# A two-recurrence pipeline on one core: state halves in 32-column matmuls, gate biases seeded by ScalarE, the shared expert dealt in half tiles

## What is computed

```python
h = tanh(h @ Wh + (x_t @ Wx + b))                # L0, simple recurrence, h0 = cond
x = x + hs
h_bar = (x_t @ Wx + b) + h @ Wh                  # L1, gated recurrence: i, f, o, g
next_c = f * prev_c + i * g
next_h = o * tanh(next_c)
x = x + hs
out = sum over experts of w_be * mask * (gelu(x @ ew1 + eb1) @ ew2 + eb2)   # L2: routed, top 2 of 4
shared = gelu(x @ sw1 + sb1) @ sw2 + sb2
x = x + out + shared
x = x + adapter(x)                               # L3: low-rank weights made from cond
```

## Time and profile before

| | |
|---|---|
| median of 3 runs | 1195.59 us (1194.09 to 1197.45) |
| profiled execution | 1194.56 us |
| its span, first to last instruction | 1192.80 us |
| mean granted TensorE clock | 0.966 |
| TensorE matmuls busy | 1144.3 us (96%), 24138 instructions |
| VectorE busy | 887.2 us (74%) |
| ScalarE busy | 515.4 us (43%) |
| GpSimd busy | 403.5 us (34%) |

### The profile page before, as it was taken

The page is one execution under the profiler, slowest core; times in us unless marked ns, Lnnn a source line. Parts: engine busy times, 40 slices in busy tenths (PEclk is TensorE's granted clock), DMA queues, the critical chain, the costliest instruction groups (busy, mean ns, idle before and its releaser), DMA issues.

```text
span 1192.8 us, 58924 instructions
## 1 busy us (share of the span) xinstructions
PE 1144.3 (96%) x24138; PEld 1033.3 (87%) x24138; DVE 887.2 (74%) x3368; ACT 515.4 (43%) x1896; POOL 403.5 (34%) x1368
## 2 busy tenths in 40 slices
PE   5999999999999999999999999789999999999898
PEld 4889889889889889999999998678888888888677
DVE  6577888887887887787787778786666666666697
ACT  3344444444454444443444343323333333333476
POOL 2654454454454454454454440181000000000021
PEclk9658999999999999999999999899999999999899
DMA  8211202202112111110000000000000000000022
GB/s 242 73 40 43 78 4 79 78 5 79 48 36 79 32 51 27 15 15 11 4 4 5 4 4 4 2 1 2 2 2 2 2 1 2 2 2 2 4 75 85
DMA packets 43282, 37.17 MB, mean 31 GB/s; under 512 B 23128, under 2 KB 38794, under 8 KB 43020
## 3 DMA queue, kind: packets, MB, share of 16 engines
q1 hardware_dynamic: 42412, 33.12, 9.2%
q10 hardware_dynamic: 608, 0.30, 0.1%
HBM read 28.42 MB, written 4.98 MB: 28 GB/s over the span
## 4 chain that ended last, share of the span: by engine, by line
PE 86%; DVE 8%; ACT 2%; issue 2%; POOL 1%; DMA 1%; SPq 0%; DVEq 0%; POOLq 0%
PE bank L1087 17%; PE bank L1088 17%; PE bank L1089 17%; PE bank L1182 16%; PE bank L1188 8%; PE bank L1156 4%; DVE seq L742 2%; PE bank L1162 2%; PE bank L1238 1%; ACT tc L529 1%; DVE LH L789 1%; PE bank L1453 1%; PE bank L1228 1%; PE bank L1425 1%; DMA WE<-in_L_cond_b 1%
## 5 line engine op out<-in xcount | busy, mean ns | idle before, releaser
L1182 PE MATMUL bank<-LH,seq 128*128 128x16 f16 x8192 | 282.0, 170 | 12.4 <-DVE LH L789 11.0
L1182 PEld LDWEIGHTS bank<-LH,seq 128*128 128x128 f16 x8192 | 250.7, 96 | 43.9 <-DVE LH L789 32.2
L1087 PE MATMUL bank<-GH,WE 128*128 128x256 f16 x768 | 209.7, 273 | 6.6 <-DVE GH L771 6.3
L534 ACT ACTIVATE gel<-bank,seq 128x256 f32<-128x256 f32 x256 | 121.5, 475 | 217.3 <-PE bank L1089 217.1
L1087 PE MATMUL bank<-XHL,WE 128*128 128x256 f16 x768 | 210.2, 274 | 3.4 <-DVE XHL L752 3.2
L769 DVE CAST GH<-gel 128x256 f16<-128x256 f32 x384 | 122.1, 318 | 120.1 <-ACT gel L534 111.9
L1088 PE MATMUL bank<-XHL,WE 128*128 128x256 f16 x768 | 210.2, 274 | 0.0
L1089 PE MATMUL bank<-XHL,WE 128*128 128x256 f16 x768 | 210.2, 274 | 0.0
L1088 PE MATMUL bank<-GH,WE 128*128 128x256 f16 x768 | 209.5, 273 | 0.0
L1089 PE MATMUL bank<-GH,WE 128*128 128x256 f16 x768 | 209.5, 273 | 0.0
L518 ACT ACTIVATE tfig<-bank 128x96 f32<-128x96 f32 x256 | 64.2, 251 | 285.9 <-PE bank L1188 285.9
(11 more groups left out here) (184 smaller groups left out, 2599.5 us busy)
## 6 DMA issues: line engine op xcount, KB each, us to landing
stage<-in_L_cond_ew SPq DMA_DIRECT2D x8, 1024.0 KB, 8.7
stage<-in_L_cond_W SPq DMA_DIRECT2D x8, 1024.0 KB, 6.1
XHL<-in_x SPq DMA_DIRECT2D x8, 512.0 KB, 9.1
out<-WE SPq DMA_DIRECT2D x16, 256.0 KB, 2.2
stage<-in_L_cond_sw SPq DMA_DIRECT2D x2, 1024.0 KB, 5.3
scratch<-rows SPq DMA_DIRECT2D x96, 8.0 KB, 2.3
stage<-in_L_cond_Wx SPq DMA_DIRECT2D x1, 1024.0 KB, 9.0
stage<-in_L_cond_Wh SPq DMA_DIRECT2D x1, 1024.0 KB, 11.1
```

Of the source, the lines that this page charges most:

```text
L534: nc.scalar.activation(gel[:, m % 2, :], banks[m % len(banks)][:, 0:256], ACT.Gelu_apprx_tanh, scale=scale, bias=bias).then_inc(s["a_g"], 1)
L1087: MM(out_, w(HI), x(HI), start=start, stop=False, skip_group_check=True)
L1182: MM(z, LW[:, h, 1, c, tile * P:(tile + 1) * P], LH[:, old, HI, c], start=False, stop=False, skip_group_check=True)
```

## The change

- `rnn_step` on TensorE: the four products high weights x high state and the four high weights x rest become four matmuls of 32 columns that read both state halves at once and write them side by side in RB (index `a`). The step has 8 matmuls instead of 12. RB now holds 8 steps, not 16, and VectorE adds the two halves (`rnn_sum`, into `rz`) before ScalarE's tanh, which reads `rz`.
- `rnn_x` runs twice per block, for 8 steps each, at the start of the simple recurrence's steps 0 and 8; the splits of its input (`split_x`) move to steps 9, 11, 13, 14 (10 to 13 in the head).
- The gate biases come in a small table `gate_bias` (eight transfers of 512 bytes, scaled once on GpSimd). ScalarE copies them into a FIG or O bank after its last reader (`seed`), and the input parts after the first two turns begin without the bias matmul.
- `cell` is gone; `fc` takes c2 of the step before, and c2 takes the half.
- ScalarE does the cell's tanh before the simple recurrence's tanh pair.
- The shared expert is dealt out in half tiles of three matmuls (`HALVES`), ahead of the input parts in TensorE's order; the second O tile set moves from step 0 to steps 3 and 5.

```diff
             def rnn_step(blk, r):
...
-                for m in range(C):
-                    for c in range(C):
-                        for h in (HI, LO):
-                            MM(z[:, m, r], RW[:, h, 1, c, m * P:(m + 1) * P], RH[:, old, HI, c],
-                               start=False, stop=False, skip_group_check=True)
+                if r % G == 0 and n > 0:
+                    rnn_x(blk, r // G)
+                if n > 0:
                     pe.wait_ge(s["a_rh"], n)
+                for m in range(C):
+                    for c in range(C):
+                        MM(z[:, 0, m, r % G], RW[:, LO, 1, c, m * P:(m + 1) * P], RH[:, old, HI, c],
+                           start=False, stop=False, skip_group_check=True)
...
-                        last = MM(z[:, m, r], RW[:, HI, 1, c, m * P:(m + 1) * P], RH[:, old, LO, c],
+                        last = MM(z[:, :, m, r % G], RW[:, HI, 1, c, m * P:(m + 1) * P], RH[:, old, :, c],
                                   start=False, stop=(c == C - 1), skip_group_check=True)
...
+            def rnn_sum(n):
+                pair = RB[:, :].rearrange("p (a m t b) -> p m t b a", a=2, m=C, t=G)[:, :, n % G]
+                dve.wait_ge(s["pe_r"], n + 1)
+                V.reduce_sum(rz[:], pair, AX_X).then_inc(s["v_rz"], 1)
...
-                V.tensor_tensor(c2[:], fc[:], ig[:], ALU.add).then_inc(s["v_c2"], 1)
-                dve.wait_ge(s["v_c2"], n + 1)
-                V.tensor_scalar(cell[:], c2[:], 0.5, None, ALU.mult)
+                V.scalar_tensor_tensor(c2[:], fc[:], 0.5, ig[:], ALU.mult, ALU.add).then_inc(s["v_c2"], 1)
+                if rnn:
+                    rnn_sum(n + U)
                 dve.wait_ge(s["a_tc"], n + 1)
...
+            def seeds(it, u, last):
+                if u % H == H - 1 and not (last and u >= U - 2 * H):
+                    seed(it * U + u + 1, FIG[u // H % 2], slice(0, 6), H, "a_fig_seed")
+                if u % G == G - 1 and not last:
+                    seed(it * U + u + 1, OB[u // G], slice(6, 8), G, "a_o_seed")
...
                     lstm_gates(it, u)
+                    lstm_cell(it, u)
                     if not last:
                         rnn_step(it + 1, u)
-                    lstm_cell(it, u)
+                    seeds(it, u, last)
...
-                    if xr and u in (4, 6, 8, 10):
+                    if xr and u in (9, 11, 13, 14):
...
+HALVES = [0, 3, 2, 2, 2, 2, 2, 3, 0, 3, 2, 3, 2, 3, 2, 1]
+O_STEPS = (3, 5)
```

More of the change, by code:

```diff
@@ L892, in block_steps @@
                 for u in range(U):
-                    lstm_step(it, u)
+                    lstm_step(it, u, not last)
                     if last and u in extras:
@@ L899, in block_steps @@
                                 split_x2(it - 1, k)
-                        for kind, m in FILL[u]:
-                            if kind == "h":
+                        for kind, m, halves in FILL[u]:
+                            if kind == "h" and C - 1 in halves:
                                 split_g(it * M + m, m)
@@ L1190, in lstm_step, with hidden, down_, shared_hidden @@
                     last.then_inc(s[done], 1)
-            def hidden(tile, w, x, bank_, free):
-                free()
-                for c in range(C):
+            def hidden(tile, w, x, bank_, free, halves=range(C)):
+                if 0 in halves:
+                    free()
+                for c in halves:
                     last = three(bank_[:, 0:256], lambda h: w(h, c), lambda h: x(h, c), c == 0, c == C - 1)
-                last.then_inc(s["pe_h"], 1)
-            def down_(tile, j, w, first, last_, ybank):
-                pe.wait_ge(s["v_gl"], tile + 1)
-                for c in range(C):
+                if C - 1 in halves:
+                    last.then_inc(s["pe_h"], 1)
+            def down_(tile, j, w, first, last_, ybank, halves=range(C)):
+                if 0 in halves:
+                    pe.wait_ge(s["v_gl"], tile + 1)
+                for c in halves:
                     last = three(ybank[:, c * 256:(c + 1) * 256], lambda h: w(h, c),
                                  lambda h: GH[:, j % 4, h], first and c == 0, last_)
-                last.then_inc(s["pe_d"], 1)
-            def shared_hidden(blk, m):
+                if C - 1 in halves:
+                    last.then_inc(s["pe_d"], 1)
+            def shared_hidden(blk, m, halves=range(C)):
                 tile = blk * M + (M + m)
@@ L1232, in low_rank, with lstm_x @@
                     last.then_inc(s["pe_w2"], 1)
[L1234 removed]
+            def lstm_x(bank_, i, tile, group, steps, fresh):
                 n = (steps.stop - steps.start) * B
                 z = bank_[:, i * n:(i + 1) * n]
[L1238 to L1239 removed]
+                if fresh:
+                    MM(z, bias_pad[:, tile * P:(tile + 1) * P], ones_pad[:, 0:n], start=(i == 0), stop=False,
+                       skip_group_check=True)
                 for c in range(C):
@@ L1316, in block_steps @@
                         logits()
+                    if not first:
+                        for kind, m, halves in FILL[u]:
+                            if kind == "h":
+                                shared_hidden(it - 1, m, halves)
+                            else:
+                                shared_down(it - 1, m, halves)
                     if u == 0:
```

146 lines of the change are left out of this document (82 added, 64 removed).

## The result

The changed kernel takes 1203.22 us, median of 9 runs (1198.61 to 1206.61). The kernel before, run beside it, takes 1195.38 us, median of 9 (1192.45 to 1199.84). The ratio is 1.0055 [1.0032, 1.0077]: slower by 0.3 to 0.8%. The forecast was 1201.6.

The account below looks back on a forecast made before the run. Two close limits bound a step: TensorE's stream (2.36 or 2.56 us) and the state-write loop (2.45). Terms 4.9 + 0 + 6.4 - 4.9 - 0.4 = +6.0 us on 1194.56 gave 1200.6, 1201.6 as median; range 1184 to 1216.

Parts of the forecast that it names:

- the head: First 16 steps of the simple recurrence: VectorE's sum and splits start the gated recurrence at 56.0 instead of 51.09, +4.9 us.
- the loop: State write through TensorE, gate tanh and VectorE to the next state write: no step can be shorter than 2.45 us.
- The stream: TensorE's matmuls: 2.5 us per block leave; 37 us over 15 blocks is the most that could come.
- the rival of doubled cost: TensorE: 32-column matmuls cost double, nothing is saved, 0.1 us more in nine steps, +14, 1215 us; chance 0.03.
- Light blocks: Blocks without weight preparation: steps sum to 42.2 us against 43.1; blocks 9 to 14 together -4.9 us.
- The delay of the state write behind the input matmuls: Steps 0 and 8: state write queued behind the sum, which waits for fourteen 128-column matmuls; 0.34 us in step 0.
- Heavy blocks: Blocks 1 to 8, with weight preparation: 46.4 us each against 45.6, +6.4 us over eight blocks.
- Step 14: Blocks 1 to 8: input difference queued behind VectorE's wait for ScalarE's rounding; 4.77 us against 2.45, +2.32.
- Step 15: Blocks 1 to 8: 2.29 us on VectorE and the addition behind it 0.75, so 3.05, +0.49.
- The clock rival: Blocks 1 to 8: TensorE's wait in step 14 lowers the clock, +2 us a block, +16 in all, 1218; chance 0.12.
- The lighter stream is what counts: Gelu and splits come early enough: 41.0 us without weight preparation, 44.5 in blocks 1 to 8, about 1180; chance 0.20.
- The sum doesn't fit: VectorE's sum of the two halves takes over 0.45 us, +0.1 a step, 1225 us or more; chance 0.05.

Follow-up runs that it names:

- e2: Changed kernel with ScalarE's seeds issued behind the gelu of their step: 1203.38 us, ratio 1.0068 to the kernel before.
- e3: Changed kernel with block 0 of the simple recurrence using 12 matmuls of 16 columns, read directly by ScalarE without VectorE's sum: 1197.13 us, ratio 1.0007.
- e6: Changed kernel with eight extra 256-column matmuls, changing no result, in step 14 of blocks 1 to 8: 1204.23 us, ratio 1.0066.
- e9: Changed kernel with the second input part at the end of step 7 and two halves dealt from step 7 to 8: 1204.65 us, ratio 1.0078.
- e8: Changed kernel with two input buffers, splits in steps 3, 5, 9, 12, one weight piece and one block sum moved, and e3's first block: 1179.71 us, ratio 0.9854.
- e11: e8 with the second input part at the end of step 7 too, as in e9: 1177.44 us, ratio 0.9847.
- e1: Changed kernel with two input buffers and the input splits in steps 3, 5, 8, 9 instead of 9, 11, 13, 14: 1195.5 us, ratio 0.9993.
- e4: Changed kernel with the merge alone undone, 12 matmuls of 16 columns per step, sum, seeds and dealing kept: 1218.39 us, ratio 1.0191.
- e10: Changed kernel with bias matmuls back in every input part and no seeds: 1209.54 us, ratio 1.0127.
- e7: Kernel before with only the shared expert dealt in half tiles ahead of the input parts: 1216.72 us, ratio 1.0178.

## Why the prediction came out right, point by point

The forecast had the mechanism: the gain ends at the loop, and what VectorE and the head add takes more than is left. That the median came within 1.6 us of it is in part luck. Up to the last state write the profiled executions differ by 10.7 us (759.80 and 770.45) where the terms add up to 6.0, so the terms miss by more than the medians do.

**The stream.** 22.0 us of TensorE's busy time went; 37 was the most that could. In blocks 9 to 13 it was 9.1, so 1.8 a block for 2.5 of work. An estimate from the rows accounts for the gap: a 16-column matmul is recorded with 170 ns and the next starts 25 ns behind it, so busy time keeps about 0.145 us before each wait, and these blocks have 19 waits where they had none. The four 32-column matmuls take 0.10, 0.025 each, what 16 columns took the earlier trace rows. That settles the rival of doubled cost: it fell. The Trainium skill ("TensorE: Matmul & The Clock Gate", section "Wait — 56ns, not 53.3ns?") gives 25 ns for 32 columns; the trace agrees.

**Light blocks** met their sum, 42.29 us (42.2), but not in each step. Means of blocks 9 to 13, measured (forecast): step 7 2.89 (2.85), steps 4, 6, 10 and 12 2.44 to 2.45 (2.45), steps 5 and 9 2.57 (2.56); but step 11 3.04 (3.3), 13 3.30 (3.15), 14 2.64 (2.45) and 1 2.75 (2.56; block 9, which begins at half clock, takes 3.27 there, the others 2.62). The errors cancel, and that is luck. The largest is the price of the input's cast in step 11. It was taken as its whole 0.72; VectorE's next operation begins 0.38 behind it:

```profile
551.50 0.75 DVE L764 CAST seq<-X 128x256 f16<-128x256 f32 x1
551.88 0.36 DVE L815 SCALAR_TENSOR_TENSOR fc<-tfig,c 128x32 f32<-128x32 f32 x1
```

The delay of the state write behind the input matmuls came with its size (0.34): the interval from 15 to 0 is 2.79, 0.34 over the loop's 2.45, and stands under step 0 in the forecast (2.84). The 0.3 us of step 7, put down to the seeds, is two waits over each other, as e2 showed: taking the seeds away leaves the sum's.

**Heavy blocks** were under-sized: +9.9 against +6.4. Step 14 came as said. VectorE's rows of block 7, with ScalarE's rounding between them:

```profile
422.76 0.39 DVE L815 SCALAR_TENSOR_TENSOR fc<-tfig,c 128x32 f32<-128x32 f32 x1
...
424.45 0.41 DVE L916 TENSOR_TENSOR low_f<-bank,low_bias 128x256 f32<-128x256 f32 x1
426.47 0.42 DVE L700 SCALAR_TENSOR_TENSOR WE<-stage,WE 128x256 f16<-128x256 f32 x1 [1.61 <-ACT WE L487]
426.82 1.23 DVE L767 TENSOR_TENSOR seq<-X,seq 128x256 f16<-128x256 f32 x1
427.68 0.39 DVE L815 SCALAR_TENSOR_TENSOR fc<-tfig,c 128x32 f32<-128x32 f32 x1
...
429.37 1.38 DVE L922 SCALAR_TENSOR_TENSOR rows<-low_f,rows 128x256 f16<-128x256 f32 x1
430.38 0.89 DVE L787 SCALAR_TENSOR_TENSOR X<-bank,X 128x512 f32<-128x512 f32 x1
431.19 0.17 DVE L815 SCALAR_TENSOR_TENSOR fc<-tfig,c 128x32 f32<-128x32 f32 x1
```

```profile
424.89 1.34 ACT L599 ACTIVATE rows<-low_f 128x256 f16<-128x256 f32 x1 [0.98 <-DVE low_f L916]
```

From fc to fc 4.92 us (forecast 4.77): 1.61 of it VectorE waits for a ScalarE that rounds, and the difference comes behind that, as written. Step 15 is the term that was off: 3.51 from fc to fc against 3.05, 0.4 a block in the mean of the state writes (3.45). I had taken 2.29 from fc to the addition, from the earlier trace rows; here it is 2.70. Of these 0.41 us, 0.13 are shown: the gate operation begins beside the still running difference and takes 0.39, not 0.19, and the state write comes 0.94 behind it, not 0.81. A small operation behind a large one was priced as if it stood alone. The other 0.28 come behind the state write, where each of three operations starts 0.07 to 0.11 us later behind the one ahead of it than in the kernel before; why is not shown. The clock has a part as well: in the 40 block ends that are sorted below, step 15 takes 3.33 us on average where the clock stays up (10 of them) and 3.54 where it is down for over 1.5 us (23). Steps 0, 10 and 13 add 0.15 each, and step 11 gives 0.3 back (3.00): there both kinds of block are under the forecast of 3.3.

**The head**: +5.8 against +4.9. The loop is the one described, ScalarE's first and last tanh and VectorE between:

```profile
24.30 0.23 ACT L520 ACTIVATE rf<-rz 128x32 f32<-128x32 f32 x1 [7.11 <-DVE rz L803]
...
53.63 0.23 ACT L520 ACTIVATE rf<-rz 128x32 f32<-128x32 f32 x1 [0.69 <-DVE rz L803]
```

```profile
40.26 0.21 DVE L803 TENSOR_REDUCE rz<-bank 128x32 f32<-128x64 f32 x1
41.19 0.49 DVE L700 SCALAR_TENSOR_TENSOR seq<-stage,seq 128x256 f16<-128x256 f32 x1 [0.72 <-ACT seq L487]
41.60 0.68 DVE L705 COPY X<-bank 128x512 f32<-128x512 f32 x1
42.20 0.21 DVE L803 TENSOR_REDUCE rz<-bank 128x32 f32<-128x64 f32 x1
```

1.94 us from sum to sum where 1.89 was forecast: 53.63 for the last tanh where 53.0 was. The sum itself took 0.21 to 0.23, at the lower end of 0.19 to 0.31.

**The clock rival.** Its event came and its price did not. I had given it 0.12 and 16 us, and had named a granted clock under 1.00 in blocks 1 to 15 as a sign of being wrong. The granted clock never left 1.00 in blocks 1 to 8 before; in the changed kernel it fell to 0.50 at the end of seven of these eight. TensorE's loads at the start of block 7 (half clock) and in step 14 (full):

```profile
386.58 0.15 PEld L1121 LDWEIGHTS bank<-XHL,WE 128*128 128x128 f16 x1
386.79 0.15 PEld L1122 LDWEIGHTS bank<-XHL,WE 128*128 128x128 f16 x1
...
425.36 0.10 PEld L1122 LDWEIGHTS bank<-GH,WE 128*128 128x128 f16 x1
425.47 0.10 PEld L1123 LDWEIGHTS bank<-GH,WE 128*128 128x128 f16 x1
```

0.21 against 0.11 between 256-column matmuls, so a fall does cost where they stand. The small matmuls hardly feel it: over the whole trace those of 16 and 32 columns start 0.027 us apart at 0.50 and 0.025 at 1.00 (medians; 64 columns 0.053 and 0.029, 256 columns 0.213 and 0.109). And it mostly passes in steps that wait for VectorE anyway. I sorted the 40 block ends of the changed kernel, e2, e3, e6 and e9 by how long the clock was at 0.50 and added the steps 15, 0, 1 and 2 of each: without a fall 11.7 us (6 cases), with one under 5 us 11.8 (19), with a longer one 12.65 (15). In the changed kernel five falls were short and two long: 5 x 0.1 and 2 x 0.95, some 2.4 us in all. That is a comparison of cases, not an edit; e6, which should have isolated it, did not change the clock. In e8 and e11, where TensorE's longest wait for LH in blocks 1 to 8 is 0.9 us, the clock fell three times and once there; so part of what they and e1 gain in the heavy blocks may be clock, and no run separates it. The Trainium skill (same page, section "Why this matters for your kernels") warns of long pauses between bursts of matmuls; here the falls came with waits for LH of at most 2.3 us.

**The other rivals.** "The lighter stream is what counts" did not hold for the kernel as changed, since the splits stood in the crowded steps; in light blocks it holds as soon as they are elsewhere (41.0 forecast, 41.15 in e1, 41.1 in e8 and e11). That its 1180 for the whole is e8's 1179.7 is chance: it had 44.5 for a heavy block and the head's loss in it, e8 has 45.3 and no loss in the head. "The sum doesn't fit" is refuted with 0.22 us. The stretch behind the recurrence was "not touched", and its +1.2 us lies within what executions of the same code differ by (429.1 to 434.2). The chances have a slip that nothing hangs on: by their own parts slower is 0.62 and same 0.18, where 0.61 and 0.19 stand.

**Where the gain went.** Undone or added alone, the parts are worth: merged matmuls -15.2 (e4), seeds -6.3 (e10), dealing in half tiles +20.6 (e7), the sum in the head +6.1 (e3). Together +5.2, against +7.8 measured. The place of the input splits costs 7.7 of what is there (e1). The parts aren't independent: in e7 the half tiles stand beside the old stream and the old places of the splits. The old dealing under the lighter stream was not run, so whether half tiles are worth having in the changed kernel stays open.

## What to carry to other kernels

When two limits lie within a few per cent of each other (here TensorE's stream at 2.56 and the loop of state, tanh and state write at 2.45), a lighter stream brings at most the difference, and it hands the lead to whatever is queued on the loop's engines. So first lay out, step by step, the free time of the engine that closes the loop, and move its bulk work into steps with room, before or together with the lighter stream; here that, with the head put back, made a kernel 26 us faster, while the change without it lost 8. Two lateness terms in one step didn't add here (step 7), and taking away one alone showed nothing; both together were not taken away. And where a small operation merges results for another engine, its place counts in both directions.

## What the runs showed of the hardware

- The granted clock fell to 0.50 at ends of blocks where TensorE's matmuls stood still for at most 2.2 us at a time, and eight extra 256-column matmuls in the pause (e6) did not prevent it.
- At a granted 0.50 the starts of 16- and 32-column matmuls are 0.027 us apart, at 1.00 0.025; of 256-column ones 0.213 and 0.109.
- ScalarE wrote 384 elements of bias into a PSUM bank in 0.47 us and 256 in 0.37; TensorE then accumulated onto them.
- A 32-element operation of VectorE, 0.19 us alone, takes 0.28 to 0.39 when it begins beside a running 256-element difference. Behind a 256-element cast of 0.75 us the next operation begins after 0.38 us.
- A reduction of 64 elements from PSUM to 32 takes 0.21 to 0.23 us, hardly more than a 32-element addition (0.19).
